# A vision tower's class token: its routing moved from the drain of the mixer to its opening, with the block limits loaded in two parts

## The reference

```python
h = token_mixer(x)                       # 16 images, 256 tokens, 256 features, plus layer norm
h = concatenate([broadcast(cls_tok), h], axis=1)        # one class row ahead of each image
h = h + scan_layer(layernorm(h))         # gates r, i; h_t = a_t * h_(t-1) + b_t; times W_out
v = layernorm(h)
logits = v @ Wr                          # 8 experts
topk_p, topk_i = top_k(softmax(logits), 2); topk_p /= topk_p.sum()
out = h + gelu_mlp_shared(v) + sum_e gate_e * gelu_mlp_e(v)       # hidden size 1024
```

## Time and profile before

| what | us |
|---|---|
| runs | 1000.47, 1002.57, 1002.79 (median 1002.57) |
| profiled execution, whole time | 1000.1 |
| its span | 998.5 |
| mean granted TensorE clock | 0.971 of full speed |
| TensorE busy | 941.2 |
| mixer phase: opening, loop, drain | to about 107, to about 480, to 543 |
| expert phase | 543 to the end |

### The profile page before, as it was taken

The page is one execution under the profiler, slowest core; times in us unless marked ns, Lnnn a source line. Parts: engine busy times, 40 slices in busy tenths (PEclk is TensorE's granted clock), DMA queues, the critical chain, the costliest instruction groups (busy, mean ns, idle before and its releaser), DMA issues.

```text
span 998.5 us, 21487 instructions
## 1 busy us (share of the span) xinstructions
PE 941.2 (94%) x6801; PEld 879.6 (88%) x6801; DVE 676.5 (68%) x2092; ACT 458.8 (46%) x1132; POOL 380.1 (38%) x470
## 2 busy tenths in 40 slices
PE   6879999999999999999886999999999999999996
PEld 4667898888898888988786999999999999999995
DVE  3687878877888777788887365645656456554643
ACT  2214344444444434444332455555555555555553
POOL 5272533334324243233535334342423435342322
PEclk9989999999999999999999899999999999999998
DMA  9305111011110011100025727372463826474222
GB/s 271 134 18 168 43 43 37 17 32 42 42 42 16 26 42 42 42 21 11 33 95 195 202 47 204 55 216 43 101 157 50 215 47 145 117 174 92 43 43 32
DMA packets 49187, 84.84 MB, mean 85 GB/s; under 512 B 6415, under 2 KB 30881, under 8 KB 49154
## 3 DMA queue, kind: packets, MB, share of 16 engines
q0 software_dynamic: 31056, 57.46, 23.6%
q1 hardware_dynamic: 18098, 26.96, 9.2%
HBM read 55.34 MB, written 29.09 MB: 85 GB/s over the span
## 4 chain that ended last, share of the span: by engine, by line
PE 59%; issue 21%; POOL 9%; DVE 7%; ACT 1%; POOLq 1%; DMA 0%; DVEq 0%; SPq 0%; ACTq 0%
PE ps_nd L764 17%; PE ps_proj L748 13%; PE ps_ri L748 6%; PE ps_nd L925 6%; PE ps_proj L832 5%; POOL out L709 5%; PE ps_ip L748 4%; PE ps_h L913 2%; PE ps_t L839 2%; PE ps_ip L898 2%; PE ps_t L1234 1%; POOL v_rows L524 1%; DVE E L1765 1%; POOL rstd L520 1%; DVE yb L1999 1%
## 5 line engine op out<-in xcount | busy, mean ns | idle before, releaser
L1593 DVE TENSOR_TENSOR GL<-g_act,GH 128x256 fp32r<-128x256 f32 (+1 forms) x416 | 171.3, 425 | 166.4 <-ACT GH L1293 164.9
L1288 ACT ACTIVATE g_act<-ps_proj,fcb 128x256 f32<-128x256 f32 (+1 forms) x272 | 129.5, 476 | 277.9 <-PE ps_proj L748 253.4
L764 PE MATMUL ps_nd<-w2h,GH 128*128 128x256 f32 x832 | 240.6, 289 | 2.4 <-DVE GL L1593 2.2
L764 PE MATMUL ps_nd<-w2h,GL 128*128 128x256 f32 x832 | 233.8, 281 | 0.0
L764 PE MATMUL ps_nd<-w2l,GH 128*128 128x256 f32 x832 | 232.9, 280 | 0.0
L764 PEld LDWEIGHTS ps_nd<-w2h,GH 128*128 128x128 f32 x832 | 156.3, 188 | 6.9 <-issue 1.8
L1293 ACT CAST GH<-g_act 128x256 fp32r<-128x256 f32 (+1 forms) x416 | 161.0, 401 | 1.1
L764 PEld LDWEIGHTS ps_nd<-w2l,GH 128*128 128x128 f32 x832 | 157.0, 189 | 0.0
L764 PEld LDWEIGHTS ps_nd<-w2h,GL 128*128 128x128 f32 x832 | 156.4, 188 | 0.0
L748 PE MATMUL ps_proj<-xh,w1h 128*128 128x256 f32 (+1 forms) x544 | 126.8, 315 | 10.1 <-DVE E L1765 8.7
L709 POOL DMA_INDIRECT out<-yb,rows_to x72 | 115.6, 1605 | 16.7 <-issue 14.0
(11 more groups left out here) (266 smaller groups left out, 1829.9 us busy)
## 6 DMA issues: line engine op xcount, KB each, us to landing
R<-v_rows SPq DMA_DIRECT2D x37, 260.0 KB, 2.7
w1h<-fc_w POOLq DMA_DIRECT2D x9, 1024.0 KB
w2h<-pj_w POOLq DMA_DIRECT2D x9, 1024.0 KB
stage<-fc_w POOLq DMA_DIRECT2D x9, 1024.0 KB, 11.4
stage<-pj_w POOLq DMA_DIRECT2D x9, 1024.0 KB, 13.9
v_rows<-tail_rows SPq DMA_DIRECT2D x8, 520.0 KB, 4.5
x<-x SPq DMA_DIRECT2D x16, 256.0 KB, 3.5
out<-yb SPq DMA_DIRECT2D x16, 256.0 KB, 2.1
```

The costliest lines, as they stand in the source:

```text
L764: last = pe.matmul(banks[a], g[:, j, a * P:(a + 1) * P], w[i][:, j, :], start=(j == 0 and q == 0), stop=(j == HT - 1 and q == 2))
L1288: act.activation(g_act[:, j % G_SLOTS, 0:width], banks[j % len(banks)][:, 0:width], ACT.Gelu_apprx_tanh, bias=fcb[i][:, j:j + 1]).then_inc ...
L1593: dve.tensor_tensor(GL[:, j, 0:width], g_act[:, j % G_SLOTS, 0:width], GH[:, j, 0:width].bitcast(F32), ALU.subtract).then_inc(gl_done, 1)
```

## The change

- CLS_AFTER becomes 0: the class row is routed ahead of image 0. Its routing is cut in separate pieces on TensorE (`cls_cols`, `cls_logits`, `cls_count`) and VectorE (`cls_v`, `cls_halves`, `cls_route`, `cls_places`, `cls_run`), all in step t = 3; ScalarE's two and GpSimd's `cls_out` go to t = 3 too. Everything that counts images behind it is raised by one (`past_cls`), and `y_out` waits for `run_ready` from image 2 on.
- `cls_v` moves from the end of VectorE's opening to the place ahead of the others.
- The spare products are gone, and TensorE loads five limits ahead of the first transposes and three behind them.

```diff
-        CLS_AFTER = NIMG - 2
-        CLS_STEP = CLS_AFTER + 2
+        CLS_AFTER = 0
 
         def past_cls(n, count):
-            return count if isinstance(n, int) and n >= CLS_AFTER else 0
+            return 0 if isinstance(n, int) and n < CLS_AFTER - 1 else count
...
# GpSimd, opening
             rows_out(3, 1)
             out_bias(3, 1)
+            cls_out(2, 0)
# GpSimd, drain
             rstd_v(18, 0)
-            cls_out(17, 1)
...
# TensorE
-        WARM = 8
+        AHEAD = 6
             def cls_c():
                 pe.wait_ge(cls_dve, 9)
-                pe.wait_ge(run_ready, CLS_AFTER)
+                pe.wait_ge(hx_done, CLS_AFTER + 2)
                 columns(CV, ps_h[:, 0, :], 2).then_inc(cls_pe, 1)
+
+            def cls_scores():
                 pe.wait_ge(cls_dve, 10)
                 pe.wait_ge(prep, 8)
...
                 after(pe, hx_done, n)
-                if live(n - 3):
+                if live(n - 2):
                     pe.wait_ge(run_ready, n - 2 + past_cls(n - 3, 1))
...
                     n = t - 3
-                    if isinstance(n, int) and n == CLS_AFTER:
-                        cls_d()
                     pe.wait_ge(vl_done, n + 1)
...
             hidden(3, 1, 0)
+            cls_cols(2, 0)
+            cls_logits(2, 0)
+            cls_count(2, 0)
             h_out(3, 1)
             logits(3, 1)
...
             gates0(16, 0)
-            cls_logits(16, 0)
             ffn_out(16, 0, 5)
...
-            limits = block_limits(pe)
-            for _ in range(WARM):
-                pe.matmul(ps_t[:, 0, :], ones_r[:], W2H[0][:, 0, :], start=True, stop=True)
+            limits = [0] + block_limits(pe, 1, AHEAD)
             transpose_rows(0)
+            limits += block_limits(pe, AHEAD, NE + 1)
             pe.wait_ge(b_done, FT * NIMG)
             experts(pe, limits, block)
 
-        def block_limits(eng):
+        def block_limits(eng, first, last):
             eng.wait_ge(bounds_ready, 1)
-            return [0] + [eng.value_load(bounds[0:1, g:g + 1], min_val=g * MIN_BLKS,
-                                         max_val=MAX_BLK - (NE - g) * MIN_BLKS)
-                          for g in range(1, NE + 1)]
+            return [eng.value_load(bounds[0:1, g:g + 1], min_val=g * MIN_BLKS,
+                                   max_val=MAX_BLK - (NE - g) * MIN_BLKS)
+                    for g in range(first, last)]
...
# ScalarE, opening and drain
             exp1(3, 1)
+            cls_high(2, 0)
+            cls_share(2, 0)
             tanh0(2, 0)
             copy_yt(3, 1)
...
             copy_u(16, 0)
-            cls_high(16, 0)
             tanh0(16, 0)
-            cls_share(16, 0)
...
# VectorE: cls_c is cut in cls_low (the low half), cls_c (to the mask and the difference)
# and cls_rows (behind the tanh), whose waits for run_ready and slots_ready go
                 dve.wait_ge(route_act, CLS_AFTER + 1)
-                dve.wait_ge(run_ready, CLS_AFTER)
-                dve.wait_ge(slots_ready, CLS_AFTER)
...
             ekv1(3, 1)
+            cls_v(2, 0)
+            cls_halves(2, 0)
+            cls_route(2, 0)
+            cls_places(2, 0)
+            cls_run(2, 0)
             h_sum(3, 1)
...
             base_sum(3, 1)
-            cls_v(2, 0)
             with dve.Fori(PEEL // 2, NIMG // 2) as pair:
...
             y_last(17, 1)
-            cls_route(16, 0)
             ratio0(18, 0)
```

More of the change, by code:

```diff
@@ L1030, in cls_attention, with cls_cols, cls_count @@
                 cls_b()
+            def cls_cols(t, par):
+                cls_c()
             def cls_logits(t, par):
-                cls_c()
+                cls_scores()
+            def cls_count(t, par):
+                cls_d()
             def step(t, par):
@@ L1584, in block @@
                 high_x(b + 1)
-            limits = block_limits(act)
+            limits = [0] + block_limits(act, 1, NE + 1)
             high_x(0)
@@ L1712, in cls_norm, with cls_chain @@
                                   ALU.subtract, ALU.mult).then_inc(cls_dve, 1)
-            def cls_c():
-                count = [0]
+            def cls_chain(done):
+                count = [done]
                 def chain(instruction):
@@ L1720, in chain, with cls_low @@
                     dve.wait_ge(route_dve, ROUTE * CLS_AFTER + count[0])
-                valid = ident[:, 0:1]
+                return count, chain
+            valid = ident[:, 0:1]
+            def cls_low():
                 dve.wait_ge(cls_act, 3)
@@ L1726, in cls_c @@
                                   ).then_inc(cls_dve, 1)
+            def cls_c():
+                count, chain = cls_chain(0)
                 chain(dve.memset(rlg[:], 0.0))
@@ L1738, in cls_c, with cls_rows @@
                                   ).then_inc(dif_done, 1)
+            def cls_rows():
+                count, chain = cls_chain(CLS_MASK)
                 dve.wait_ge(route_act, CLS_AFTER + 1)
-                dve.wait_ge(run_ready, CLS_AFTER)
-                dve.wait_ge(slots_ready, CLS_AFTER)
                 chain(dve.tensor_copy(CV[0:1, FIRST_E:FIRST_E + 1], ridx[0:1, 0, 0:1]))
@@ L2011, in cls_v, with cls_halves, cls_places, cls_run @@
                 cls_norm()
+            def cls_halves(t, par):
+                cls_low()
             def cls_route(t, par):
                 cls_c()
+            def cls_places(t, par):
+                cls_rows()
+            def cls_run(t, par):
+                cls_d()
             def bias_wait(t, par):
```

## The result

| | before | changed |
|---|---|---|
| median of 8 runs each, us | 1000.44 (996.56 to 1002.79) | 1008.17 (1006.37 to 1009.35) |
| ratio, 95% interval | 1 | 1.0072 [1.0057, 1.0087] |
| span of the profiled execution | 998.5 | 1006.8 |
| mean granted TensorE clock | 0.971 | 0.965 |

What follows compares the result with a forecast made beforehand. VectorE, then GpSimd, then TensorE were taken to bound the opening, TensorE the loop (94% busy). Opening +12.9, drain -4.7, transition -2.0 gave +6.2 us, set on 1001.5: 1007.7 us, range 1000.5 to 1011.5.

Steps and rivals of the forecast that it cites:

- chain ahead of L913: Opening: the class routing chain delays image 2's output product by its full length, 8.2 us (7.7 to 9).
- L913 at the low clock: Opening: after over 6 us of TensorE idling, image 2's output product runs at 1.2 GHz, 1.5 us longer (0 to 1.7).
- class scatters: Opening, GpSimd: two class scatters ahead of image 3's rstd count in full, 2.5 us (1.25 to 2.8).
- clock at the loop's entry: Loop's entry: TensorE idles longer, lengthening the low-clock stretch already there; 0.7 us added (-1.5 to +1.7).
- drain: Drain: without class routing the logits start 4.6 us sooner, plus 0.1 for the clock; gain 4.7 us (3.2 to 6.3).
- transition: Limits to first expert product: five limits, then transposes, no spare products; 2.0 us gained (1.3 to 2.7).
- clock behind the transition: First expert products: the 4.1 us of low clock moves along, spare products or not; counted as nothing.
- three limits ... run beside them and end at about 551.8: Transition: three limits, 2.3 us on TensorE's sequencer, outlast the halves of X (551.0), so the first product starts at 551.8.
- 1: Rival: the opening swallows most of its lateness in TensorE's waits, so not slower; 1002.3, or 1000.0 at upper bounds; 23%.
- 2: Rival: more low clock behind image 2's output product (1.5 us) and at the loop's entry (1.7); 1010.9; 15%.
- 4: Rival: the drain gives nothing, as something else holds its logits; +10.9 us, 1012.4; 2%.
- 3: Rival: the spare products counted towards the clock's return; without them the first expert products cost 2.1 us more, 1009.8; 10%.

Runs made afterwards that it cites:

- e1: Changed kernel with the two class scatters earlier on GpSimd's queue, behind rstd_u(3, 1) instead of out_bias(3, 1); 1005.71 us, ratio 1.0051.
- e8: The kernel before, unedited, traced once more; one run, 1001.16 us.
- e4: Changed kernel with the old transition: eight limits and eight spare products ahead of the transposes again; 1008.65 us, ratio 1.0081.
- e2: Kernel before with the new transition alone: five limits, transposes, three limits, no spare products; 998.89 us, ratio 0.9977.
- e12: e9 with 34 spare products: six ahead of each of the five limits before the transposes, four behind the last; 993.48 us, ratio 0.9904.
- e9: e5 with the class norm moved behind h_norm(2, 0) and the additions to the running counts ahead of h_sum(3, 1); 999.2 us, ratio 0.9967.
- e10: e9 with eight spare products between the first five limits and the transposes; 995.44 us, ratio 0.9946.
- e3: Changed kernel with eight spare products back between the first five limits and the transposes; 1006.48 us, ratio 1.0061.
- e11: e2 with eight spare products between the first five limits and the transposes; 998.68 us, ratio 0.9974.
- e5: Changed kernel with class pieces laid into waits of steps 2 and 3, the count in another bank, scatters early; 997.56 us, ratio 0.9969.

## Why the prediction was right, and where it was off

It was right in sign and size, and in the main by its own steps. Each term, predicted and measured (means of the four traces without e1 where the table above has several; for the last two terms, all seven traces without spare products against the first trace, e8 and e4):

| term | predicted | measured |
|---|---|---|
| chain ahead of L913 | 8.2 (7.7 to 9) | 84.42 - 76.50 = 7.9 |
| L913 at the low clock | 1.5 (0 to 1.7) | 3.79 - 1.93 = 1.9 |
| class scatters | 2.5 | 39.60 - 37.14 = 2.5 |
| clock at the loop's entry | 0.7 | 25.24 - 24.58 = 0.7 |
| loop | 0 | +0.8, by chance or not |
| drain | -4.7 (-3.2 to -6.3) | 45.78 - 50.98 = -5.2 |
| transition | -2.0 (-1.3 to -2.7) | 7.80 - 10.53 = -2.7 |
| clock behind the transition | 0 | 11.65 - 11.15 = +0.5, ranges overlap |
| sum | +6.2 | +6.3; by the ratios +7.2 and +6.5 |

**Opening.** 12.9 predicted; in the first pair of traces image 4's output product stood 12.89 later (141.06, 153.95). The signs named beforehand came: L914 at 85.09 for 85.6, TensorE's waits of 3.25 and 2.78 (6.0 together) with the last named for `run`, rstd's wait 5.08 for 4.8, the loop's first hidden product at 128.46 for 129. L913 went past its upper bound: the step "L913 took about 1.75" scaled too small a number by a ratio from L925, where its own row says 1.89; all of it ran at 1.2 GHz and its 1.89 doubled. That is the first mis-sized term, by 0.4. It fell on a chain 0.3 us shorter than named, so that the 12.9 came out to the hundredth is luck. The 0.7 at the loop's entry is right in size but had another case in mind: "a longer one" at 0.7 and "if it doubles" at 1.7. It doubled, from 3.5 to about 7 us of low clock in all four traces with the late rstd (first the kernel before, then the changed one), and cost 0.7; VectorE was busy for 5.45 of these 6 us:

```profile
127.50:133.50 6.00, 5.04 (x11) 2.97 (x12) 5.45 (x29) 0.47 (x1) 4.02 (x6) 0.50 0.00 0
```

**Drain.** The wait fell from 3.20 to 0.54, where under 0.5 was named. Between the logits of image 13 and 14 the first pair shows only 3.5 (25.02 to 21.49), but e8 took 27.09 for the same stretch of the same program. The whole drain gave 3.07 in the first pair, below the stated 3.2, and 5.2 over all traces, inside 3.2 to 6.3. As one program differs by 3.4 us there, that 4.7 came so near to 5.2 is in part luck.

**Transition.** 2.7 instead of 2.0. The step that failed: "three limits ... run beside them and end at about 551.8". They were not late. Without them the prediction had the first product at 551.0, and the bounds' start before, 543.18, with the 7.80 us that were measured gives 550.98. The transposes and the two halves of X take 2.5 us from the start of the transposes to the first product (558.71 to 561.23), the wait before that product was for xl, and the three reads fitted beside. Against this 0.7 stands a term I had at nothing, the clock: from the first expert product to the second round 10.8 to 11.4 us with the old form (before, e8, e4), 10.8 to 12.1 in the seven traces without spare products (mean 11.65).

**Rivals.** 1 (the opening swallows it) is out: the first hidden product was 11.99 us late, against the 9.7 at which it decides; 2 (more low clock in the opening) had its condition but not its price: the low clock lasted from 79.5 to 89 and came doubled at the loop's entry, and nothing beyond the charged 1.9 and 0.7 was lost. 4 is out by the drain. 3 isn't shown: the 2.1 us did not come, and the 0.5 us of the means is less than the spread of one kind (e2 took 11.38 without spare products, e8 11.44 with them). The Trainium skill (TensorE: Matmul & The Clock Gate, Why this matters for your kernels) wants TensorE busy ahead of the work; e12's rows agree in the strict form (no wait over 1.58 us, PEclk 1.00 throughout, 9.54 us to the second round), while eight products behind an idle gap of 3.8 us were followed by the full clock in two traces of three, and in the old form, behind 6.1 us (the kernel before, e8, e4), in none of three.

**What stays open.** The output product of image 2 starts anywhere within 1.9 us in kernels that are the same up to there, and the loop varies by 1.7; low-clock stretches come in one execution and not in another, and no run here says what decides. Where they fall matters as much: in the first trace of the kernel before (first block of rows) the clock was full from 33 on and TensorE waited 3.13 us for U, and the low clock came behind that wait (0.57 from 38.5 to 42.5); in e8 (second block) it came ahead of it, the wait shrank to 0.45, and the output product of image 2 started 1.45 us sooner. In these two traces the low clock cost less where it fell on a wait.

```profile
33.00:38.50 5.50, 2.63 (x12) 1.33 (x11) 1.88 (x8) 0.72 (x4) 3.43 (x4) 1.00 0.69 236
```

```profile
33.00:38.50 5.50, 5.50 (x17) 3.31 (x16) 1.96 (x7) 0.72 (x4) 3.40 (x4) 0.53 0.79 280
```

A class routing that is wholly hidden in the opening was not reached: the three traces of e9's opening enter the loop at 119.44 (e9), 116.93 (e10) and 118.63 (e12), on the mean 2.8 us later than the 115.56 of the four with the class in the drain.

## What to carry to other kernels

Before moving work into a wait, ask what that wait is for: VectorE's 5.16 us were spent waiting for TensorE, and the moved chain both started from TensorE's columns and fed TensorE's next product, so it came on top of the wait instead of filling it. Moved work is hidden only when its pieces are spread over waits that end for other reasons, and when the small pieces others wait for go first (rstd ahead of the scatters, by 2.5 us here; `run` ahead of `h_sum` ended a wait of 3.44, though no time shows it). And where TensorE must idle while its sequencer reads registers, spare products between the reads kept its clock in e12's trace, at no cost in time.

## What the runs showed of the hardware

- Reading a register on TensorE's sequencer and its matmuls ran beside each other: five reads and 24 products of 3.28 us took 4.19 us in e12, five reads alone 3.88 to 3.92 (e3, e10, e11).
- A norm of 1x256 values on VectorE took 2.37 us while GpSimd subtracted 128x1024 halves, and 0.39 to 0.46 elsewhere; two norms of 128x256 took 3.67 beside such a subtraction and 0.73 elsewhere. The Trainium skill (SBUF — State Buffer, SBUF: two separate sides) names a port pair that GpSimd and some VectorE instructions take in turn, for whole instructions; the pair of rows in e5 fits that, and no run here shows that it is this port.
- Granted clock is a property of the execution as much as of the program: in the drain alone the kernel before took 48.81 us in one trace and 52.19 in another. A forecast or an explanation to 3 us should not rest on one trace of each kernel.
